# Row fetches by byte offset, sixteen registers a load, three buffers a queue, and more tiles for the SyncE and ScalarE queues

## The chip, the cores and the metric

The kernel runs on one core of one Trainium2 chip. The metric is the device time of one execution in microseconds (us). The engines are PE (TensorE), DVE (VectorE), ACT (ScalarE), POOL (GpSimd) and SP (SyncE); SP only issues DMAs and waits. ACT, SP and POOL each have an instruction queue of their own from which they also issue DMAs.

## What is computed

A graph layer for 12,500 nodes of 256 features and 200,000 edges: a layer norm, then a graph convolution and a linear attention, which are both added to x, then a second layer norm and a mixture of eight experts (two for a token).

```python
xn = layernorm(x)
HW = xn @ W
AHW = segment_sum(edge_weight[:, None] * HW[dst], src, num_segments=12500)
q, k = elu(q) + 1, elu(k) + 1                      # linear attention, 8 heads
out = (q @ (k^T v)) / max(q . sum(k), 1e-6) @ Wproj + bproj
x = x + (AHW + b) + out
x = x + moe(layernorm(x))                          # 8 experts, top 2
```

The change touches the segment sum (called the aggregation below): for every edge a row of HW is read and added, weighted, to the row of its node.

## The kernel before

The edges are first sorted into blocks of 128 nodes and laid out in 1660 tiles of 128 edges; four tiles are a set, so there are 415 sets (TSETS). The rows of HW lie in DRAM as h_table, 12,544 rows of 256 floats, 1024 bytes each. For each tile the 128 rows that its edges name have to come into SBUF, one on each partition. Then PE multiplies a selection matrix, made by DVE from the records of the tile, with these rows (function aggregate, L1266), and DVE adds the result to the block in acc (set_turn, add_tile, L1831).

The rows of most tiles are brought by POOL with one indirect DMA a tile, a gather, into message, which holds four sets (gather_set, L758). POOL may begin set k when PE has done set k - 4. Some tiles, always the last of a set, are brought in another way: SP and ACT each fetch such a tile with 128 single DMAs, one a row, into fetched (fetch_rows, L455). Set SP_SET + 16 i has a tile of SP, 25 in all, and set ACT_SET + 20 i has one of ACT, 19 in all; POOL makes three gathers in these sets and four in the others, 1616 in all. The numbers of the rows lie as integers in fetch_row, one partition for each fetched tile; a queue loads eight of them into registers with one instruction (load_offsets, L47), bounds them (L48), and issues eight DMAs whose source is given by a register.

A tile is fetched in portions. SP's tile i is spread over the 16 sets from 8 + 16 i (fetch_span), 8 rows a set; ACT's over 20 sets, 6.4 rows a set, cut to whole rows. Each portion is issued in loads of eight and a rest. Two buffers a queue are used in turn; the queue waits until PE has used the tile two before.

The fetches are written by hand into the order of work of two long loops, 49 units each. In the K/V part a unit is three sets: PE projects K and V of a pair of blocks between them (project_kv, L1307), ACT takes the exponential and the RELU of K (split_k, L1005 and L1006) and copies V (L1015), DVE joins them (activate, L1954), and PE sums k^T v (context, L1321). Between the sets' work ACT issues the portion of its tile for three sets, after its copy of V. SP waits until V of the last unit but one is made, issues the DMA of xt for a unit (bring_xt, L566), and then its portion for three sets. In the mix part a unit is five sets: PE projects Q (L1377), ACT takes exponential and RELU of Q (split_q, L1034 and L1035), DVE divides (L1998 to L2002), PE multiplies and adds x (L1397 and L1399), and SP brings xt and x (L566, bring_x, L578) and then its portion for five sets. Four sets between the two parts (WEIGHT_FIRST) fold the weights; the last eleven follow the mix part. Later stages, the gate and the experts, aren't touched.

Of the kernel before, what the change touches and what calls it, by code (L numbers as in the profile page):

```python
# [43 lines left out]
def load_offsets(eng, name, row, first, count, top):  # L44

    registers = name if isinstance(name, list) else [eng.alloc_register(f"{name}{i}") for i in range(count)]
    eng.load(registers, row[0:1, first:first + count] if isinstance(first, int) else row[0:1, DynSlice(first, count)])  # L47
    return [eng.snap(r, min_val=0, max_val=top) for r in registers]  # L48


def gps_layer(nc, x, src, dst, edge_weight, gnn_W, gnn_b, mix_Wq, mix_Wkv, mix_Wproj, mix_bproj,
# [1 line left out]
    import concourse.bass as bass  # L53
    from concourse import mybir

    F32, BF16, I32 = mybir.dt.float32, mybir.dt.bfloat16, mybir.dt.int32
    ALU, ACT, AX = mybir.AluOpType, mybir.ActivationFunctionType, mybir.AxisListType.X
    ds = bass.ds
    Offset = bass.IndirectOffsetOnAxis

    P = 128
    N, C = x.shape
    E = src.shape[0]
    KC = C // P
    NB = -(-N // P)
# [3 lines left out]
    EXPERTS, _, HID = ffn_W1.shape  # L69
# [23 lines left out]
    SET, SETS, RING = 4, 4, 8  # L93
# [6 lines left out]
    CONTEXT_SETS, MIX_SETS = 3, 5  # L100
    CONTEXT_FIRST = RING
# [6 lines left out]
    XGROUPS = -(-NB // XG)  # L108
    assert MIX_END < TSETS and TSETS * SET <= TC and 2 * PAIRS == NB and PAIRS % 2 and RING == 2 * SETS

    SP_SPAN, SP_SET = 16, 27
    ACT_SPAN, ACT_SET = 20, 37
    SP_FETCHED = (TSETS - 1 - SP_SET) // SP_SPAN + 1
    ACT_FETCHED = (TSETS - 1 - ACT_SET) // ACT_SPAN + 1
    SP_TILE, ACT_TILE = SP_SET * SET + SET - 1, ACT_SET * SET + SET - 1
    fetched_of = {SP_SET + i * SP_SPAN: (0, i) for i in range(SP_FETCHED)}
    fetched_of.update({ACT_SET + i * ACT_SPAN: (1, i) for i in range(ACT_FETCHED)})
    assert len(fetched_of) == SP_FETCHED + ACT_FETCHED and max(fetched_of) < TSETS
    FETCHED = SP_FETCHED + ACT_FETCHED

    TURN = 7
    TB = 2 * TURN
# [18 lines left out]
    h_table = nc.dram_tensor("h_table", (NB * P, C), F32, kind="Internal").ap()  # L141
# [6 lines left out]
    with ExitStack() as whole:  # L148
        def sem(name):
            return whole.enter_context(nc.semaphore(name))  # L150

        def sb(name, shape, dtype, scope=whole):
            return scope.enter_context(nc.sbuf_tensor(name, shape, dtype))
# [84 lines left out]
        early = ExitStack()  # L238
# [9 lines left out]
        message = sb("message", [P, SETS, SET, C], F32, early)  # L248
        lane = sb("lane", [P, 1], F32, early)
        select = sb("select", [P, 2, SET, P], F32, early)  # L250
        fetched = sb("fetched", [P, 2, 2, C], F32, early)
        fetch_f = sb("fetch_f", [P, FETCHED], F32, early)
        fetch_row = sb("fetch_row", [FETCHED, P], I32, early)
        inputs = ExitStack()
# [3 lines left out]
        found_a = sb("found_a", [P, PART_MAX * P], I32, inputs)  # L258
        found_b = sb("found_b", [P, PART_MAX * P], I32, inputs)
        inputs.close()  # L260
        mix_w = sb("mix_w", [P, KC, C], F32, early)
        ksum = sb("ksum", [P, KC, P], F32, early)
        ctx_t = sb("ctx_t", [P, KC, P], F32, early)
# [45 lines left out]
        bank = [whole.enter_context(nc.psum_tensor(f"bank{i}", [P, 512], F32)) for i in range(8)]  # L309
# [81 lines left out]
        s_fetch_f = sem("s_fetch_f")  # L391
        s_fetch_psum = sem("s_fetch_psum")
        s_fetch_row = sem("s_fetch_row")
        s_fetched = [[sem(f"s_fetched{q}_{i}") for i in range(2)] for q in range(2)]
        s_acc_made = sem("s_acc_made")
        s_select = sem("s_select")
        s_agg = sem("s_agg")
# [41 lines left out]
        LISTED = [64 * len(range(i, K, 4)) for i in range(4)]  # L439
        PARTS = [(0, 1), (1, 5), (5, 9), (9, RSEG)]  # L440

        def gathered_of(k):

            return sum(SET - (n in fetched_of) for n in range(k % SETS, k + 1, SETS))

        def fetch_rows(eng, registers, queue, i, first, end):

            if i >= 2 and first == 0:
                eng.wait_ge(s_agg, {place: k for k, place in fetched_of.items()}[queue, i - 2] + 1)
            at = i + SP_FETCHED * queue  # L450
            for a in range(first, end, 8):
                n = min(8, end - a)
                rows_at = load_offsets(eng, registers[0:n], fetch_row[at:at + 1, :], a, n, NB * P - 1)
                for j in range(n):
                    eng.dma_start(fetched[a + j:a + j + 1, queue, i % 2, :], h_table[ds(rows_at[j], 1), :]).then_inc(s_fetched[queue][i % 2], 16)  # L455

        def fetch_span(eng, registers, queue, span, first_set, end_set):

            for i in range([SP_FETCHED, ACT_FETCHED][queue]):
                begins = CONTEXT_FIRST + i * span  # L460
                first, end = max(first_set, begins), min(end_set, begins + span)
                if first < end:
                    fetch_rows(eng, registers, queue, i, P * (first - begins) // span, P * (end - begins) // span)
# [29 lines left out]
        def _(sp):  # L493
# [83 lines left out]
                else:  # L577
                    sp.dma_start(x_in[:, pair % 2, :, :], x_pairs[pair:pair + 1, :, :, :].rearrange("a p u c -> p (a u) c")).then_inc(s_x_in[pair % 2], 16)  # L578

            row_registers = [sp.alloc_register(f"row_{i}") for i in range(8)]  # L580

            def fetch_ahead(first, end):
                fetch_span(sp, row_registers, 0, SP_SPAN, first, end)
# [252 lines left out]
        def _(act):  # L836
            steps = Steps(act, s_act)
            for r in range(-(-SEG // 4)):
                n = min(4, SEG - 4 * r) * P
# [48 lines left out]
            for k in range(-(-M // BANK_BATCHES)):  # L888
                first, last = k * BANK_BATCHES, min((k + 1) * BANK_BATCHES, M)
# [4 lines left out]
            for i in range(TURNED):  # L894
# [5 lines left out]
                else:  # L900
                    a = (i - SEG) * 4 * P
                    n = min(4 * P, NCOL - a)
# [95 lines left out]
            copy_weights()  # L998


            def split_k(unit, first=False):
                act.wait_ge(s_k_psum, unit + 1)
                if not first:
                    act.wait_ge(s_k, unit)
                act.activation(exp_kq[:, :], bank[4][:, :], ACT.Exp)  # L1005
                act.activation(relu_kq[:, :], bank[4][:, :], ACT.Relu).then_inc(s_k_split, 1)  # L1006
                act.wait_ge(s_v_psum, unit + 1)
                if not first:
                    act.wait_ge(s_ctx, unit)
                made = bank[5][:, :].rearrange("p (u h c) -> p u h c", u=2, h=KC)  # L1010
                if first:
                    act.activation(v_sb[:, 0, :, 0:P], made[:, 0, :, :], ACT.Copy)
                    act.activation(v_sb[:, 1, :, 0:P], made[:, 1, :, :], ACT.Identity, scale=row_ok[:, 1, 0:1]).then_inc(s_v, 1)
                else:
                    act.activation(v_sb[:, :, :, 0:P], made, ACT.Copy).then_inc(s_v, 1)  # L1015
            act.wait_ge(s_late, 2)
            row_registers = [act.alloc_register(f"row_{i}") for i in range(8)]

            def fetch_ahead(first, end):
                fetch_span(act, row_registers, 1, ACT_SPAN, first, end)  # L1020
            for unit in range(PAIRS):
                split_k(unit, first=unit == 0)
                if unit == 0:
                    act.wait_ge(s_fetch_row, 1)
                fetch_ahead(CONTEXT_FIRST + unit * CONTEXT_SETS, CONTEXT_FIRST + (unit + 1) * CONTEXT_SETS)
            fetch_ahead(WEIGHT_FIRST, MIX_FIRST)

            def split_q(g, first=False):
# [83 lines left out]
        def _(pe):  # L1112
# [12 lines left out]
            for b in range(M):  # L1125
# [3 lines left out]
                for g in range(GS):  # L1129
                    at = 2 * (b % BANK_BATCHES * GS + g)  # L1130
# [119 lines left out]
            for i in range(-(-TC // 512)):  # L1250
                n = min(512, TC - 512 * i)
# [3 lines left out]
            def aggregate(k, slot, first=False):  # L1255
                pe.wait_ge(s_select, k + 1)
                pe.wait_ge(s_message[slot % SETS], 16 * gathered_of(k))
                if k in fetched_of:
                    queue, nth = fetched_of[k]
                    pe.wait_ge(s_fetched[queue][nth % 2], 16 * P * (nth // 2 + 1))  # L1260
                if not (first and slot < 2):
                    pe.wait_ge(s_added, k - 1)
                for j in range(SET):
                    ps = bank[(slot % 2) * 2 + j // 2][:, (j % 2) * C:(j % 2 + 1) * C]
                    rows_of = fetched[:, queue, nth % 2, :] if k in fetched_of and j == SET - 1 else message[:, slot % SETS, j, :]
                    last = nc.tensor.matmul(ps, select[:, slot % 2, j, :], rows_of, start=True, stop=True)  # L1266
                last.then_inc(s_agg, 1)

# [26 lines left out]
            pe.wait_ge(s_fetch_f, 1)  # L1295
            nc.tensor.transpose(bank[6][0:FETCHED, 0:P], fetch_f[:, :], ident[:, :]).then_inc(s_fetch_psum, 1)
            pe.wait_ge(s_joined, RSEG)
# [247 lines left out]
        def _(dve):  # L1545
            steps = Steps(dve, s_dve)
            V = nc.vector
# [255 lines left out]
            for m in range(M):  # L1803
# [8 lines left out]
                def between(i):  # L1812
                    if m + 1 < M:
                        find_third(m * STEP + STEP + 1 + i // 3, i % 3)
# [48 lines left out]
            for nth, (a, b) in enumerate(PARTS):  # L1863
# [23 lines left out]
                if nth == 0:  # L1887
                    for i in range(-(-TC // 512)):
                        n = min(512, TC - 512 * i)
# [11 lines left out]
            steps.done(V.tensor_copy(fetch_f[:, 0:SP_FETCHED], records[:, SP_TILE:SP_TILE + (SP_FETCHED - 1) * SP_SPAN * SET + 1:SP_SPAN * SET, 0]))  # L1901
            steps.done(V.tensor_copy(fetch_f[:, SP_FETCHED:FETCHED], records[:, ACT_TILE:ACT_TILE + (ACT_FETCHED - 1) * ACT_SPAN * SET + 1:ACT_SPAN * SET, 0]))
            steps.settle()
# [1 line left out]
            for k in range(RING - 1, RING):  # L1905
                set_turn(k)
            dve.wait_ge(s_fetch_psum, 1)
            V.tensor_copy(fetch_row[:, :], bank[6][0:FETCHED, 0:P]).then_inc(s_fetch_row, 1)

            def block_stats(first_block, j):  # L1910
                steps.done(V.bn_stats(stats[:, j, :], acc[:, first_block + j, 0:C]))
# [53 lines left out]
            for slot in plain_sets(WEIGHT_FIRST, SETS):  # L1965
                if slot == 0:
                    dve.wait_ge(s_ctx, PAIRS)
                    for h in range(KC):
                        at = h * (P + 1)
# [324 lines left out]
```

## Time and profile before

| | us |
|---|---|
| median of three runs | 3787.94 |
| lowest and highest of them | 3780.83, 3790.05 |
| the profiled execution | 3789.91 |
| its span, first to last instruction | 3788.2 |
| mean granted TensorE clock (of 1) | 0.905 |

The profile is of one execution. Times in it count from the start of the span. An engine is busy while an instruction of it computes; instructions that issue DMAs, load registers or wait aren't counted as busy, but the views by line list them, under SPq and ACTq, with their own durations. Idle time is put down to what ended it; "issue" there is a wait for nothing that the profile shows.

### The profile page before, as it was taken

The numbers are of one execution on the slowest core, as the hardware profiler recorded it, in microseconds if no ns is written. First come the engines' busy times: TensorE is split into PE (matmuls) and PEld (weight loads), VectorE is DVE, ScalarE is ACT, GpSimd is POOL, SyncE is SP. The second block draws the span as 40 slices with busy tenths as digits, with TensorE's granted clock in tenths as the row PEclk, the third lists the DMA queues.
The fourth block names the chain that finished last, engine by engine and source line by source line (L and its number), as shares of the span: only waits on it lengthen the run. The fifth ranks groups of instructions, "written<-read, shape, count | busy, mean of one in ns | idle before, by whom it ended". The sixth has DMA issues, their size and how long they took to land. (4 is left out here: it accounts for less than half of the span.)

```text
span 3788.2 us, 70898 instructions
## 1 busy us (share of the span) xinstructions
PE 2773.6 (73%) x16403; PEld 2280.8 (60%) x16408; DVE 2523.3 (67%) x6338; ACT 637.1 (17%) x1335; POOL 2557.6 (68%) x2387
## 2 busy tenths in 40 slices
PE   1457667587777776777777676676663999999998
PEld 1346666366556665555555555555431888888887
DVE  8999999465555555777777777777683544454444
ACT  8312223311111110000000000000032222122221
POOL 7347777677777777777777777777717478744444
PEclk9987878899999999888888889988876999999999
DMA  5957775744444444444444444444383455544443
GB/s 175 303 165 229 232 222 163 228 117 128 127 128 125 127 125 125 130 130 130 130 130 127 127 131 130 130 130 127 107 254 107 74 121 122 111 79 71 71 73 56
DMA packets 357535, 522.47 MB, mean 138 GB/s; under 512 B 59192, under 2 KB 278332, under 8 KB 357180
## 3 DMA queue, kind: packets, MB, share of 16 engines
q0 software_dynamic: 128832, 269.87, 28.0%
q1 hardware_dynamic: 172947, 191.01, 16.6%
q10 hardware_dynamic: 55401, 57.82, 4.9%
q8 instruction: 105, 1.72, 0.2%
q14 instruction: 250, 2.05, 0.2%
HBM read 378.21 MB, written 140.28 MB: 137 GB/s over the span
## 5 line engine op out<-in xcount | busy, mean ns | idle before, releaser
L758 POOL DMA_INDIRECT message<-h_table,records x1616 | 1551.4, 960 | 509.6 <-issue 494.3
L1266 PE MATMUL bank<-message,select 128*128 128x256 f32 x3232 | 919.6, 434 | 552.6 <-issue 268.1
L1266 PEld LDWEIGHTS bank<-message,select 128*128 128x128 f32 x3232 | 660.3, 213 | 767.4 <-issue 367.7
L1823 DVE TENSOR_SCALAR select<-iota_n,records 128x128 f32<-128x128 f32 x1660 | 596.9, 360 | 489.0 <-PE bank L1266 472.2
L1831 DVE TENSOR_TENSOR acc<-acc,bank 128x256 f32 x1660 | 682.6, 411 | 10.0 <-PE bank L1266 6.3
L802 POOL DMA_INDIRECT out<-acc,row_of x224 | 352.2, 1572 | 356.7 <-DVE acc L2239 230.9
L723 POOL DMA_INDIRECT lists<-placed,dest_i x300 | 349.1, 1164 | 200.9 <-ACT placed L935 106.0
L1506 PE MATMUL bank<-w,acc 128*128 x1792 | 407.6, 381 | 8.0 <-DVE acc L2223 7.9
L1493 PE MATMUL bank<-fx_t,acc 128*128 128x256 f32 x1792 | 408.0, 381 | 1.6 <-ACT fx_t L1086 1.6
L1493 PEld LDWEIGHTS bank<-fx_t,acc 128*128 128x128 f32 x1792 | 342.3, 191 | 49.1 <-issue 2.1
L1506 PEld LDWEIGHTS bank<-w,acc 128*128 128x128 f32 x1792 | 333.0, 191 | 50.6 <-issue 9.4
L2235 DVE TENSOR_TENSOR acc<-bank,table 128x256 f32<-128x256 f32 x224 | 84.5, 419 | 336.1 <-PE bank L1506 187.7
L791 POOL DMA_INDIRECT x_sorted<-acc,token_pos x196 | 192.1, 980 | 128.9 <-DVE acc L1940 69.5
L1034 ACT ACTIVATE exp_kq<-bank 128x512 f32<-128x512 f32 x49 | 29.3, 597 | 1155.2 <-PE bank L1377 1111.8
L2223 DVE TENSOR_SCALAR acc<-bank,table 128x256 f32<-128x256 f32 x448 | 190.6, 478 | 44.4 <-PE bank L1493 35.3
L1307 PE MATMUL bank<-w_cat,xt_in 128*128 128x256 f32 x784 | 199.3, 400 | 5.1 <-DMA xt_in<-xt_dram 5.1
L1307 PEld LDWEIGHTS bank<-w_cat,xt_in 128*128 128x128 f32 x784 | 161.2, 206 | 32.9 <-DMA xt_in<-xt_dram 6.6
L1954 DVE SCALAR_TENSOR_TENSOR act_kq<-exp_kq,relu_kq 128x512 f32<-128x512 f32 x98 | 68.0, 694 | 169.3 <-ACT relu_kq L1006 167.0
L1086 ACT ACTIVATE fx_t<-bank 128x512 f32<-128x512 f32 x112 | 66.9, 597 | 643.3 <-PE bank L1480 643.3
L2000 DVE RECIPROCAL relu_kq<-exp_kq 128x512 f32<-128x512 f32 x49 | 164.3, 3353 | 1.7
L1175 PE MATMUL bank<-place_bf,hot_t 98*128 98x4 bf16 x1575 | 48.6, 165 | 130.7 <-DVE hot_t L1731 127.7
L1194 PE MATMUL bank<-hot_w,hot_q 128*128 128x128 bf16 x1575 | 140.6, 266 | 0.0
(315 smaller groups left out, 3512.8 us busy)
## 6 DMA issues: line engine op xcount, KB each, us to landing
fetched<-h_table SPq DMA_DIRECT2D x3200, 1.0 KB
fetched<-h_table ACTq DMA_DIRECT2D x2432, 1.0 KB
rows<-block_dram SPq DMA_DIRECT2D x75, 514.5 KB
acc<-x_sorted SPq DMA_DIRECT2D x112, 260.0 KB, 2.8
message<-h_table,records POOLq DMA_INDIRECT x1616
xt_in<-xt_dram SPq DMA_DIRECT2D x98, 256.0 KB
x_sorted<-blank_rows ACTq DMA_DIRECT2D x42, 390.0 KB
lists<-zeros_list SPq DMA_DIRECT2D x8, 1664.0 KB, 15.4
```

What stands on the lines that cost most here:

```text
L723: pool.indirect_dma_start(out=lists, out_offset=Offset(ap=dest_i[:, c, i:i + 1], axis=0), in_=placed[:, c % 4, i * G8 * PIECES:(i + 1) * G ...
L758: pool.indirect_dma_start(out=message[:, k % SETS, j, :], out_offset=None, in_=h_table, in_offset=Offset(ap=records[:, k * SET + j, 0:1], ...
L791: pool.indirect_dma_start(out=x_sorted[half], out_offset=Offset(ap=token_pos[:, b, k:k + 1], axis=0), in_=acc[:, b, :], in_offset=None).th ...
L802: pool.indirect_dma_start(out=out, out_offset=Offset(ap=row_of[:, ring, j:j + 1], axis=0), in_=fy[:, slot, j, :], in_offset=None, compute_ ...
L1266: last = nc.tensor.matmul(ps, select[:, slot % 2, j, :], rows_of, start=True, stop=True)
L1307: last = nc.tensor.matmul(ps[:, u * C:(u + 1) * C], xt_in[:, half, k, u * P:(u + 1) * P], w_cat[:, k, cols:cols + C], start=(k == 0), stop ...
L1493: last = nc.tensor.matmul(bank[2 + 2 * slot + h // 2][:, h % 2 * 2 * P:(h % 2 + 1) * 2 * P], w1_now[:, slot, k * HID + h * P:k * HID + (h ...
L1506: last = nc.tensor.matmul(bank[6 + slot][:, j * C:(j + 1) * C], hid_t[:, slot, k, j * P:(j + 1) * P], w2_flat[:, ds(expert + k * C, C)], s ...
L1823: return V.tensor_scalar(select[:, k % 2, j, :], iota_n[:, :], records[:, k * SET + j, 1:2].bitcast(F32), records[:, k * SET + j, 2:3].bit ...
L1831: return V.tensor_tensor(to, to, ps, ALU.add)
L2000: steps.done(V.reciprocal(relu_kq[:, :], exp_kq[:, :]))
L2223: last = V.tensor_scalar(hid_t[:, slot, h, :], bank[2 + 2 * slot + h // 2][:, h % 2 * 2 * P:(h % 2 + 1) * 2 * P], table_flat[:, ds(expert ...
```

## The change

The numbers of the rows are multiplied by 1024 when DVE writes fetch_row, so that fetch_row holds byte offsets. The row DMAs read 1024 bytes of a flat byte view of h_table at such an offset, and write a byte view of fetched. One load brings up to sixteen registers. There are three buffers a queue, and the wait is for the tile three before. SP's tiles are spread over 12 sets, every twelfth set having one (33 tiles), ACT's over 14 (28 tiles, the first in set 36); POOL makes 1599 gathers. In the K/V part ACT issues the portion of a unit's first set between the RELU of K and the copy of V, and that of the other two behind the copy.

```diff
-    SP_SPAN, SP_SET = 16, 27
-    ACT_SPAN, ACT_SET = 20, 37
+    SP_SPAN, SP_SET = 12, 27
+    ACT_SPAN, ACT_SET = 14, 36
...
+    FETCHED, FETCH_RING = SP_FETCHED + ACT_FETCHED, 3
...
+        fetched = sb("fetched", [P, 2, FETCH_RING, C], F32, early)
...
+        ROW_BYTES = 4 * C
+        h_bytes = h_table.rearrange("n c -> (n c)").bitcast(U8)
...
-            if i >= 2 and first == 0:
-                eng.wait_ge(s_agg, {place: k for k, place in fetched_of.items()}[queue, i - 2] + 1)
+            if i >= FETCH_RING and first == 0:
+                eng.wait_ge(s_agg, {place: k for k, place in fetched_of.items()}[queue, i - FETCH_RING] + 1)
...
-            for a in range(first, end, 8):
-                n = min(8, end - a)
-                rows_at = load_offsets(eng, registers[0:n], fetch_row[at:at + 1, :], a, n, NB * P - 1)
+            for a in range(first, end, 16):
+                n = min(16, end - a)
+                byte_at = load_offsets(eng, registers[0:n], fetch_row[at:at + 1, :], a, n, (NB * P - 1) * ROW_BYTES)
                 for j in range(n):
-                    eng.dma_start(fetched[a + j:a + j + 1, queue, i % 2, :], h_table[ds(rows_at[j], 1), :]).then_inc(s_fetched[queue][i % 2], 16)
+                    eng.dma_start(fetched[a + j:a + j + 1, queue, i % FETCH_RING, :].bitcast(U8),
+                                  h_bytes[ds(byte_at[j], ROW_BYTES)].unsqueeze(0)).then_inc(s_fetched[queue][i % FETCH_RING], 16)
...
-            def split_k(unit, first=False):
+            def split_k(unit, between, first=False):
...
                 act.activation(relu_kq[:, :], bank[4][:, :], ACT.Relu).then_inc(s_k_split, 1)
+                between()
                 act.wait_ge(s_v_psum, unit + 1)
...
-            row_registers = [act.alloc_register(f"row_{i}") for i in range(8)]
+            row_registers = [act.alloc_register(f"row_{i}") for i in range(16)]
...
-                fetch_ahead(CONTEXT_FIRST + unit * CONTEXT_SETS, CONTEXT_FIRST + (unit + 1) * CONTEXT_SETS)
+                first_set = CONTEXT_FIRST + unit * CONTEXT_SETS
+
+                def first_rows():
+                    if unit == 0:
+                        act.wait_ge(s_fetch_row, 1)
+                    fetch_ahead(first_set, first_set + 1)
+                split_k(unit, first_rows, first=unit == 0)
+                fetch_ahead(first_set + 1, first_set + CONTEXT_SETS)
...
-            V.tensor_copy(fetch_row[:, :], bank[6][0:FETCHED, 0:P]).then_inc(s_fetch_row, 1)
+            V.tensor_scalar(fetch_row[:, :], bank[6][0:FETCHED, 0:P], float(ROW_BYTES), None, ALU.mult).then_inc(s_fetch_row, 1)
```

## Rows read from the trace of the kernel before

**Rows 1.** Head of the page: the span and its instructions.
```profile
span 3788.2 us, 70898 instructions
```

**Rows 2.** Table by stage: busy us (instructions) of each engine, clock, DMA share.
```profile
760.00:1492.00 732.00, 543.39 (x2389) 445.52 (x2388) 402.63 (x1265) 81.78 (x149) 554.81 (x578) 0.94 0.43 125
1520.00:2700.00 1180.00, 832.83 (x3073) 648.27 (x3071) 871.97 (x2160) 53.38 (x97) 894.96 (x935) 0.88 0.43 129
```

**Rows 3.** Page, costliest groups: busy us, mean ns, idle us before, releaser.
```profile
L758 POOL DMA_INDIRECT message<-h_table,records x1616 | 1551.4, 960 | 509.6 <-issue 494.3
```

**Rows 4.** Timeline of POOL, mix part: start us, duration us [idle before].
```profile
1999.14 0.95 POOL L758 DMA_INDIRECT message<-h_table,records  x1 [0.30 <-issue]
...
2027.98 0.95 POOL L758 DMA_INDIRECT message<-h_table,records  x1 [0.30 <-issue]
```

**Rows 5.** Lines L1005 and L1034: duration ns min/median/max, first and last start.
```profile
L1005 ACT ACTIVATE exp_kq<-bank x49: 597/597/599, 763.4 to 1466.9; 128x512 f32<-128x512 f32 x49
...
L1034 ACT ACTIVATE exp_kq<-bank x49: 597/597/598, 1497.4 to 2675.8; 128x512 f32<-128x512 f32 x49
```

**Rows 6.** Waits, 780 to 1490 us: us in total, times, longest.
```profile
ACT exp_kq L1005 <- issue: 471.2, 38, 13.8
```

**Rows 7.** Waits of SP's queue, 780 to 2700 us.
```profile
SPq L578 <- PE bank L1399: 70.5, 36, 4.1
SPq L566 <- PE bank L1307: 25.5, 21, 2.4
SPq L47 <- PE bank L1266: 5.1, 8, 0.8
SPq L472 <- PE bank L1399: 3.2, 1, 3.2
```

**Rows 8.** Timeline of SP's queue in three short windows of the mix part.
```profile
2012.41 0.23 SPq L455 DMA_DIRECT2D fetched<-h_table  x1
...
2012.41 0.64 SPq L455 DMA_DIRECT2D fetched<-h_table  x2
...
2015.49 4.64 SPq L455 DMA_DIRECT2D fetched<-h_table  x9
```

**Rows 9.** Line L455, all row fetches: duration ns, first and last start.
```profile
L455 SPq MOVE fetched<-h_table x3200: 29/29/38, 758.1 to 2691.4; - x189
L455 SPq DMA_DIRECT2D fetched<-h_table x3200: 224/228/332, 758.1 to 2691.5; - x189
L455 SPq FUSED_REGOPS  x2800: 37/37/48, 758.5 to 2691.3; - x187
...
L455 ACTq DMA_DIRECT2D fetched<-h_table x2432: 234/235/552, 766.6 to 2620.5; - x188
```

**Rows 10.** Line L47, SP's loads of eight registers: duration ns.
```profile
L47 SPq TENSOR_LOAD <-fetch_row x400: 692/788/1037, 757.0 to 2687.4; - x134
```

**Rows 11.** Timeline of ACT's queue in two short windows of the mix part.
```profile
2015.29 3.20 ACTq L455 DMA_DIRECT2D fetched<-h_table  x8
...
2015.29 6.11 ACTq L455 DMA_DIRECT2D fetched<-h_table  x9
```

**Rows 12.** Line L47, single loads of ACT: rows 76, 19, 92, 16, 123.
```profile
L47 ACTq TENSOR_LOAD <-fetch_row x1: 750/750/750, 821.0 to 821.0; - x1
...
L47 ACTq TENSOR_LOAD <-fetch_row x1: 2003/2003/2003, 777.6 to 777.6; - x1
...
L47 ACTq TENSOR_LOAD <-fetch_row x1: 598/598/598, 830.1 to 830.1; - x1
...
L47 ACTq TENSOR_LOAD <-fetch_row x1: 1012/1012/1012, 774.8 to 774.8; - x1
...
L47 ACTq TENSOR_LOAD <-fetch_row x1: 1481/1481/1481, 854.1 to 854.1; - x1
```

**Rows 13.** Line L47, ACT's loads from 1520 to 2700 us.
```profile
L47 ACTq TENSOR_LOAD <-fetch_row x191: 762/2046/2222, 1521.8 to 2618.9; - x191
```

More of the change, by code:

```diff
@@ L54, in gps_layer @@
     from concourse import mybir
-    F32, BF16, I32 = mybir.dt.float32, mybir.dt.bfloat16, mybir.dt.int32
+    F32, BF16, I32, U8 = mybir.dt.float32, mybir.dt.bfloat16, mybir.dt.int32, mybir.dt.uint8
     ALU, ACT, AX = mybir.AluOpType, mybir.ActivationFunctionType, mybir.AxisListType.X
@@ L118, in gps_layer @@
     assert len(fetched_of) == SP_FETCHED + ACT_FETCHED and max(fetched_of) < TSETS
-    FETCHED = SP_FETCHED + ACT_FETCHED
+    FETCHED, FETCH_RING = SP_FETCHED + ACT_FETCHED, 3
     TURN = 7
@@ L250, in gps_layer @@
         select = sb("select", [P, 2, SET, P], F32, early)
-        fetched = sb("fetched", [P, 2, 2, C], F32, early)
         fetch_f = sb("fetch_f", [P, FETCHED], F32, early)
@@ L393, in gps_layer @@
         s_fetch_row = sem("s_fetch_row")
-        s_fetched = [[sem(f"s_fetched{q}_{i}") for i in range(2)] for q in range(2)]
+        s_fetched = [[sem(f"s_fetched{q}_{i}") for i in range(FETCH_RING)] for q in range(2)]
         s_acc_made = sem("s_acc_made")
@@ L578, in bring_x @@
                     sp.dma_start(x_in[:, pair % 2, :, :], x_pairs[pair:pair + 1, :, :, :].rearrange("a p u c -> p (a u) c")).then_inc(s_x_in[pair % 2], 16)
-            row_registers = [sp.alloc_register(f"row_{i}") for i in range(8)]
+            row_registers = [sp.alloc_register(f"row_{i}") for i in range(16)]
             def fetch_ahead(first, end):
@@ L1021, in _ @@
             for unit in range(PAIRS):
-                split_k(unit, first=unit == 0)
-                if unit == 0:
-                    act.wait_ge(s_fetch_row, 1)
-                fetch_ahead(CONTEXT_FIRST + unit * CONTEXT_SETS, CONTEXT_FIRST + (unit + 1) * CONTEXT_SETS)
+                first_set = CONTEXT_FIRST + unit * CONTEXT_SETS
[5 more added lines that the diff above has]
+                fetch_ahead(first_set + 1, first_set + CONTEXT_SETS)
             fetch_ahead(WEIGHT_FIRST, MIX_FIRST)
@@ L1259, in aggregate @@
                     queue, nth = fetched_of[k]
-                    pe.wait_ge(s_fetched[queue][nth % 2], 16 * P * (nth // 2 + 1))
+                    pe.wait_ge(s_fetched[queue][nth % FETCH_RING], 16 * P * (nth // FETCH_RING + 1))
                 if not (first and slot < 2):
@@ L1264, in aggregate @@
                     ps = bank[(slot % 2) * 2 + j // 2][:, (j % 2) * C:(j % 2 + 1) * C]
-                    rows_of = fetched[:, queue, nth % 2, :] if k in fetched_of and j == SET - 1 else message[:, slot % SETS, j, :]
+                    rows_of = fetched[:, queue, nth % FETCH_RING, :] if k in fetched_of and j == SET - 1 else message[:, slot % SETS, j, :]
                     last = nc.tensor.matmul(ps, select[:, slot % 2, j, :], rows_of, start=True, stop=True)
```

## The prediction

> **What bounds the kernel now.** The profiled execution took 3789.9 us, its span is 3788.2 [rows 1], 2 us above the median of the three runs (3780.83 to 3790.05); sums are made against 3789.9, and 0.3%, about 11 us, is what a measurement can tell from no change. No engine is full over the span, so I look at the stage that the change touches. The table by stage [rows 2] shows two parts: 760 to 1492 us, where the K/V pass runs beside the aggregation, three sets a unit, and 1520 to 2700 us, where the mix pass does, five sets a unit. POOL is counted busy 76% in both. But before 1606 of 1616 gathers POOL waited for nothing that the profile shows, in all 494.3 us [rows 3]: 0.95 us of gather and 0.30 us to the next; the 24 from 1999.14 to 2027.98 us follow each other in 28.84 / 23 = 1.254 us [rows 4]. POOL is therefore the bound: a set of four gathers is 5.0 us. The first exponentials of the units confirm the pace: 48 steps in 763.4 to 1466.9 us, 14.66 us a unit, and 48 in 1497.4 to 2675.8, 24.55 us [rows 5]. By gathers alone it would be (12 - 0.34) x 1.254 = 14.6 and (20 - 0.56) x 1.254 = 24.4.
>
> What stands close behind POOL decides this change. SP and ACT each issue one DMA a row for the tiles that POOL leaves to them, and the same two queues also bring x and run the activations that the units wait for. ACT's exponential came late from its own queue in 38 of the K/V units [rows 6]: PE had long made K. SP waited for others only 70.5 + 25.5 + 5.1 + 3.2 = 104 us of the 1912 us in both parts [rows 7]. Both queues are some 95% full already, and the change gives them 33 and 28 tiles in place of 25 and 19.
>
> **What it takes from POOL.** 61 tiles in place of 44: 17 gathers fewer, 17 x 1.254 = 21.3 us [rows 4]. If POOL stays the bound that is the whole gain: 3789.9 - 21.3 = 3769. Its pace would be (12 - 3/12 - 3/14) x 1.254 = 14.47 us a K/V unit and (20 - 5/12 - 5/14) x 1.254 = 24.11 us a mix unit. SP's and ACT's work in a unit must fit into these.
>
> **What a row costs SP and ACT now.** On SP, two row DMAs in a run end 0.64 us after the first begins, one takes 0.23 [rows 8]: a row each 0.41 us, 0.228 of it the DMA, the rest two register instructions (37 and 29 ns) and the gaps around them [rows 9]. Nine rows take 4.64 us, the ninth being the first of the next load [rows 8], so a load of eight with its rows takes 4.64 - 0.26 = 4.38 us: 8 x 0.41 = 3.28, 0.79 for the load [rows 10], and 0.31 for the instruction that checks the values and the gaps. On ACT a row step is 0.39 us, and eight with their load take 6.11 - 0.47 = 5.64 [rows 11]: 3.12, 2.05 for the load, 0.47 for the rest (its first DMA after a load is longer).
>
> Why does the same load take 0.79 us on SP and 2.05 on ACT? Because of where it starts. With 16 sets a tile SP starts always at a multiple of 8 rows. With 20 sets ACT's third set boundary is row 19. Its load of eight from row 76 takes 0.75 us, from row 19 2.00; four from row 92 0.60, three from row 16 1.01, five from row 123 1.48 [rows 12]. I read it as 0.4 us a load and 0.2 us for each step, where a step brings four registers if the start and what is left are multiples of four, and else one: 0.4 + 2 x 0.2 = 0.8; 0.4 + 8 x 0.2 = 2.0; 0.6; 1.0; 1.4. It fits all five, and the median of 2.046 over ACT's loads of the mix part [rows 13], most of which start at such rows.
>
> **The change, part by part.**
>
> Byte offsets: the row number no longer has to be multiplied for each DMA. Bounds: nothing goes (0.41 and 0.39 us stay), or both register instructions go (the DMA with one gap, 0.228 + 0.045 = 0.27, and 0.265). I take the middle, the 37 ns instruction and its gap gone: 0.33 on SP, 0.325 on ACT, since the 29 ns MOVE stands before every row DMA and no row of the trace says that it serves the multiplication. The DMA itself keeps its 0.228 us: it moves the same 1024 bytes.
>
> Sixteen registers a load: the 0.4 us falls on 16 rows, not 8, but the steps stay. A load from a good row costs 0.4 + 4 x 0.2 = 1.2 us, from another 0.4 + 16 x 0.2 = 3.6. For the check of sixteen values I add 0.1 us: 0.41 on SP, 0.57 on ACT beside the load.
>
> Twelve and fourteen sets: three sets of twelve are 32 rows, so in the K/V part SP starts at good rows. Five sets are 53.3 rows: mix units start at rows 53, 106, 32, 85, 10 and so on. Counted from the code, 88 of SP's 196 loads there start at a multiple of four, and 2614 rows need 1750 steps (before: 1960 rows, 490 steps). On ACT one set is 9.14 rows; in the K/V part, 1344 rows, 147 loads (the split into one and two sets keeps it at three a unit), 1068 steps.
>
> Third buffer: the wait is then for a set 17 before the first fetched one, and was 13 before. It spares waits of bursts, not work. The multiplication moves into an instruction of DVE that ran once anyway; nothing.
>
> ACT's split: one set's rows stand between the RELU and the copy of V. This takes no time off the queue; what is queued behind them is the copy, and PE waits for it in the unit's third set.
>
> **The sums.** Checked on the old kernel: SP in the mix part 1960 x 0.41 + 245 x (0.4 + 0.31) + 490 x 0.2 + 49 x 0.9 (xt and x) = 1120 us; 49 x 24.55 less SP's waits of some 100 is 1103. It fits.
>
> New, SP in the mix part: 2614 x 0.33 = 863, 196 x (0.4 + 0.41) = 159, 1750 x 0.2 = 350, 49 x 0.9 = 44: 1416 us, 28.9 a unit, where 24.55 went before: 49 x 4.35 = 213 us more. ACT there: 2204 rows, 159 loads, 1571 steps, 49 x 1.2 of activations: 716 + 154 + 314 + 59 = 1243, 25.4 a unit, hidden behind SP. New, ACT in the K/V part: 437 + 147 x 0.97 = 143 + 214 + 59 = 853, 17.4 a unit against 14.66: 134 us more. SP there: 1568 x 0.33 + 98 x 0.81 + 392 x 0.2 + 25 = 699, 14.3 a unit, hidden. The queues don't make it up later: xt of the next unit stands behind the rows on SP, the exponential behind them on ACT, and PE, DVE and at last POOL, which needs the messages' buffers back, wait for those. 3789.9 + 213 + 134 = **4137 us**.
>
> **Rivals.**
>
> *No register instruction goes.* SP mix 1072 + 553 = 1625, 33.2 a unit, +422; ACT K/V 524 + 416 = 940, 19.2, +222: 4434 us. For it: the trace shows no row DMA at a register without both.
>
> *Both go.* SP mix 706 + 553 = 1259, 25.7, +56; ACT K/V 356 + 416 = 772, 15.75, +54: 3900 us. Against it: the MOVE.
>
> *Loads cost the same however many registers and wherever they start* (the other side). With 0.8 us a load, as SP's now, SP mix is 863 + 196 x 1.21 + 44 = 1144, 23.3 a unit, under 24.11; ACT K/V 437 + 147 x 1.37 + 59 = 697, 14.2, under 14.47. POOL stays the bound: 3769. It decides from about 0.9 us a load. Against it stand the loads of 0.6 to 2.0 us [rows 12]; for it, that no load of sixteen is in the trace. The Trainium skill, "DMA: Bandwidth & Descriptors", section "Latency and other measured facts", gives tensor_load a floor of about 600 ns and unrolls four times to share it; by a floor alone, longer loads are the right cure and the time is this rival's 3769. The trace bears out the 0.6 us for four registers, but not that it is all.
>
> *The register row is no longer well placed.* fetch_f, four bytes a fetched tile, grows from 44 x 4 = 176 to 61 x 4 = 244 bytes a partition, and fetch_row lies behind it. Were tiles packed without rounding, SP's K/V loads would go singly too (+217, mix +386): about 4390. Against it: tiles of 4 bytes stand ahead of it now, and loads at multiples of four are quick.
>
> **How the numbers follow.** Forecast 0.50 (its own range 4060 to 4220: 0.02 us on a row is 50 us); no instruction gone 0.18; both 0.10; misplaced row 0.02; POOL stays the bound 0.16; a balance within 11 us 0.04. Slower 0.80, same 0.04, faster 0.16. The range leaves out the faster case: 3785 to 4450.
>
> **What would show it.** In the profile after: POOL's gathers no longer each 1.254 us but in groups with idle time that PE ended; the mix unit 28.9 us and the K/V unit 17.4; SP's row step 0.33 us; SP's loads of sixteen at 1.2 us in the K/V part, and many near 3.6 in the mix part. Wrong if the loads of sixteen stay near 1 us everywhere, or the row step falls under 0.27.

## The result: 4046 us, and the profile after

The changed kernel takes 4046.15 us (median of four runs, 4042.91 to 4046.38), the kernel before 3788.51 (four runs, 3780.83 to 3790.05): ratio 1.0682, 95% interval 1.0664 to 1.0701. It is slower, as forecast, by 258 us where 347 were forecast. The time lies in the stated range, and 14 us below the range of the case that was forecast (4060 to 4220). The mean granted TensorE clock was 0.864 and had been 0.905; the two queues below set the pace with hardly a wait, so it is not PE's speed that was lost.

In the page of the changed kernel, first its head, then two of the costliest groups (busy us, mean ns of one, idle us before, releaser). They answer to [rows 1, 3].

```profile
span 4044.7 us, 69846 instructions
...
L762 POOL DMA_INDIRECT message<-h_table,records x1599 | 1534.3, 960 | 786.6 <-issue 758.3
...
L1386 PE MATMUL bank<-xt_in,w_cat 128*128 128x256 f32 x392 | 145.6, 536 | 280.5 <-DMA xt_in<-xt_dram 280.5
```

POOL has 17 gathers fewer and 17 us less to do, but stands idle 277 us longer. The profile puts that down to "issue". By the start times in the trace, 71 gathers begin more than 2 us after the one before (one did in the kernel before), 280 us over the pace of 1.254 in all, and 68 of them begin 0.8 us after the end of the last matmul of a set: POOL waited for PE to free its buffers. PE waits 280.5 us for xt in the mix part: those are the DMAs that SP issues between its rows.

The first exponential of each unit, L1009 in the K/V part and L1043 in the mix part, by the view of a line (first and last start at the end). They answer to [rows 5].

```profile
L1009 ACT ACTIVATE exp_kq<-bank x49: 597/597/599, 766.0 to 1550.5; 128x512 f32<-128x512 f32 x49
...
L1043 ACT ACTIVATE exp_kq<-bank x49: 597/597/599, 1583.9 to 2947.1; 128x512 f32<-128x512 f32 x49
```

A K/V unit takes (1550.5 - 766.0) / 48 = 16.34 us and was 14.66, a mix unit (2947.1 - 1583.9) / 48 = 28.40 and was 24.55. That is 48 x 1.69 = 81 and 48 x 3.85 = 185 us. The stretch behind the last of these exponentials is 14.8 us shorter (1097.6 for 1112.4), the stretches before and between them 5.5 longer: 81 + 185 - 15 + 5.5 = 256.5, the whole difference of the two spans.

What SP's queue waited for from 1584 to 2947 us, the mix part (us in total, times, longest), answering to [rows 7]:

```profile
SPq L47 <- PE bank L1275: 5.1, 6, 1.3
SPq L582 <- PE bank L1408: 0.2, 1, 0.2
```

5 us in 1363: SP is the bound there. The waits in the K/V part, 780 to 1550 us:

```profile
ACT exp_kq L1009 <- issue: 437.2, 42, 11.8
...
PE bank L1330 <- ACT v_sb L1020: 211.9, 47, 7.3
```

There it is ACT: 42 exponentials came late from its own queue (38 did before [rows 6]), and PE waits in 47 of the units for V, whose copy now stands behind rows. By the start times in the trace, ACT's queue stood 8.8 us in all at its activations in these 770 us, and 80 us in the kernel before (780 to 1466): it is full now, and was some 88% full, not the 95% that the prediction gave both queues.

How the rows are issued, first by line L458 (durations in ns, min/median/max), then by SP's timeline in two windows that begin together (16 DMAs, and 17, the last of the next load). They answer to [rows 8, 9].

```profile
L458 SPq MOVE fetched<-h_table x4224: 29/29/38, 759.0 to 2973.2; - x192
L458 SPq DMA_DIRECT2D fetched<-h_table x4224: 224/228/488, 759.1 to 2973.2; - x192
L458 ACTq MOVE fetched<-h_table x3584: 29/29/35, 766.0 to 2953.0; - x200
L458 ACTq DMA_DIRECT2D fetched<-h_table x3584: 234/235/550, 766.1 to 2953.3; - x200
```

```profile
2016.65 5.13 SPq L458 DMA_DIRECT2D fetched<-h_table  x16
...
2016.65 7.19 SPq L458 DMA_DIRECT2D fetched<-h_table  x17
```

The FUSED_REGOPS of 37 ns is gone, the MOVE and the 228 ns of the DMA stayed. A row costs (5.13 - 0.23) / 15 = 0.327 us in this load, 0.322 in its undisturbed steps, and 0.333 on the mean of SP's mix part, where some steps, mostly those next to a load, are longer.

The loads, line L47, of SP's and ACT's queue from 780 to 1550 us, then of both from 1584 to 2947 us, answering to [rows 10, 13]:

```profile
L47 SPq TENSOR_LOAD <-fetch_row x97: 1149/1227/1451, 785.6 to 1544.7; - x97
...
L47 ACTq TENSOR_LOAD <-fetch_row x141: 765/1264/3844, 781.1 to 1548.7; - x141
...
L47 SPq TENSOR_LOAD <-fetch_row x189: 779/1391/3802, 1584.1 to 2941.8; - x189
...
L47 ACTq TENSOR_LOAD <-fetch_row x158: 597/3212/4003, 1583.9 to 2938.1; - x158
```

In the K/V part all of SP's loads of sixteen start at multiples of four and take 1.2 us; elsewhere loads of sixteen reach 3.6 to 4.0.

### The profile page after: what moved, and what is told of

The parts are those of the page before. It is cut to its first block and busy times, and to the rows that moved or that the text cites. A ratio compares the mean times of both kernels' runs of the same rounds, so it can differ in the third digit from the quotient of the medians.

```text
span 4044.7 us, 69846 instructions
## 1 busy us (share of the span) xinstructions
PE 2831.3 (70%) x16403; PEld 2348.9 (58%) x16408; DVE 2522.6 (62%) x6338; ACT 639.2 (16%) x1335; POOL 2538.8 (63%) x2370
## 5 line engine op out<-in xcount | busy, mean ns | idle before, releaser
L762 POOL DMA_INDIRECT message<-h_table,records x1599 | 1534.3, 960 | 786.6 <-issue 758.3
L1275 PE MATMUL bank<-message,select 128*128 128x256 f32 x3198 | 871.6, 424 | 78.3 <-DVE acc L1840 52.3
L1275 PEld LDWEIGHTS bank<-message,select 128*128 128x128 f32 x3198 | 682.3, 218 | 227.5 <-DVE select L1832 96.0
L1386 PE MATMUL bank<-xt_in,w_cat 128*128 128x256 f32 x392 | 145.6, 536 | 280.5 <-DMA xt_in<-xt_dram 280.5
L1995 DVE TENSOR_TENSOR acc<-acc,bank 128x512 f32<-128x512 f32 x49 | 33.7, 687 | 428.0 <-ACT relu_kq L1044 427.9
L1386 PEld LDWEIGHTS bank<-xt_in,w_cat 128*128 128x128 f32 x392 | 100.6, 268 | 315.9 <-DMA xt_in<-xt_dram 297.4
L1330 PE MATMUL bank<-v_sb,act_kq 128*128 128x129 f32 x388 | 95.1, 422 | 216.0 <-ACT v_sb L1020 215.6
L1043 ACT ACTIVATE exp_kq<-bank 128x512 f32<-128x512 f32 x49 | 29.3, 597 | 1339.4 <-PE bank L1386 893.3
L1330 PEld LDWEIGHTS bank<-v_sb,act_kq 128*128 128x128 f32 x388 | 82.3, 313 | 234.2 <-issue 234.2
L1316 PE MATMUL bank<-w_cat,xt_in 128*128 128x256 f32 x784 | 189.0, 384 | 0.0
```

The source lines that it names most:

```text
L762: pool.indirect_dma_start(out=message[:, k % SETS, j, :], out_offset=None, in_=h_table, in_offset=Offset(ap=records[:, k * SET + j, 0:1], ...
L1316: last = nc.tensor.matmul(ps[:, u * C:(u + 1) * C], xt_in[:, half, k, u * P:(u + 1) * P], w_cat[:, k, cols:cols + C], start=(k == 0), stop ...
L1386: last = nc.tensor.matmul(bank[4][:, o * C:(o + 1) * C], w_cat[:, k, 2 * C + o * P:2 * C + (o + 1) * P], xt_in[:, half, k, :], start=(k == ...
```

## The experiments

Each ran in turns with the kernel before on one chip; the ratio is to that. The units are worked out from the first and last exponential of each run, as above.

| run | us | ratio (95%) | K/V unit | mix unit |
|---|---|---|---|---|
| the change | 4046.2 | 1.0682 (1.0664 to 1.0701) | 16.34 | 28.40 |
| e1 portions at multiples of 4 | 3767.5 | 0.9947 (0.9931 to 0.9964) | 14.42 | 24.35 |
| e2 kernel before, odd starts | 4118.3 | 1.0876 (1.0858 to 1.0895) | 17.07 | 29.02 |
| e3 no split | 4018.0 | 1.0611 (1.0593 to 1.0629) | 15.81 | 28.42 |
| e4 old spans | 3788.3 | 1.0005 (0.9995 to 1.0014) | 14.56 | 24.52 |
| e5 SP 12, ACT 20 sets | 3978.3 | 1.0506 (1.0488 to 1.0523) | 14.49 | 28.79 |
| e6 SP 16, ACT 14 sets | 3904.3 | 1.0310 (1.0293 to 1.0328) | 16.42 | 25.43 |
| e7 multiples of 16, 10 and 12 sets | 4102.4 | 1.0835 (1.0817 to 1.0853) | 17.06 | 28.85 |
| e8 = e1 with two buffers | 3767.4 | 0.9949 (0.9933 to 0.9966) | 14.40 | 24.45 |
| e9 = e1 with loads of eight | 3861.4 | 1.0192 (1.0175 to 1.0209) | 15.13 | 25.74 |
| e10 = e1 with row numbers | 4127.7 | 1.0887 (1.0869 to 1.0906) | 17.13 | 29.18 |

**e1, good starts.** The changed kernel; only the borders of the portions are cut down to multiples of four rows.

```diff
-                    fetch_rows(eng, registers, queue, i, P * (first - begins) // span, P * (end - begins) // span)
+                    fetch_rows(eng, registers, queue, i, P * (first - begins) // span // 4 * 4, P * (end - begins) // span // 4 * 4)
```

> The changed kernel, but each portion begins and ends at a row that is a multiple of four; as many rows and tiles. Theory (the start of a load decides, SP is the bound in the mix part, ACT in the K/V part): SP in the mix part needs 2616 x 0.322 + 196 x 0.81 + 654 steps x 0.2 + 44 = 1176 us, 24.0 us a unit, ACT in the K/V part 12.9, both under POOL's 24.1 and 14.5; so 3765 to 3800 us, SP's long loads at 1.2 us and none at 3.6. Rival (39% more rows are too many for these queues, however they are loaded): 4000 us or more. Rival (the rows between RELU and the copy of V make V late): the K/V unit stays at 16.3, 3850 to 3880 us.

Measured: 3767.5 us, 0.9947 of the kernel before: 0.5% under it, little but clear of the interval, and 279 us under the changed kernel. Its loads by line L47, and then POOL's gathers in its table of groups:

```profile
L47 SPq TENSOR_LOAD <-fetch_row x297: 557/1225/1472, 756.1 to 2676.3; - x149
L47 ACTq TENSOR_LOAD <-fetch_row x284: 583/1202/1477, 761.3 to 2658.2; - x142
```

```profile
L762 POOL DMA_INDIRECT message<-h_table,records x1599 | 1533.3, 959 | 504.7 <-issue 488.9 <-DVE records L1895 12.2 <-PE bank L1275 3.7
```

No load is over 1.48 us, and POOL is idle 504.7 us in place of 786.6. As many rows, tiles and loads on SP (ACT has 284 loads for 309): the 279 us between this kernel and the changed one come from where portions begin and end. The split stays in it, and V no longer comes late.

But SP has no slack left. Its queue's waits from 780 to 2700 us:

```profile
SPq L47 <- PE bank L1275: 9.4, 10, 1.3
SPq L582 <- PE bank L1408: 0.5, 1, 0.5
SPq L570 <- PE bank L1316: 0.2, 1, 0.2
```

That is 10 us in 1920. With 0.333 us a row, not the 0.322 of the expectation, SP needs 24.6 us a mix unit, half a us over POOL's 24.1: here SP and POOL are about level.

**e2, bad starts for the kernel before.** Everything as before the change, but the rows stand one integer further right in fetch_row.

```diff
-        fetch_row = sb("fetch_row", [FETCHED, P], I32, early)
+        fetch_row = sb("fetch_row", [FETCHED, P + 4], I32, early)
...
-                rows_at = load_offsets(eng, registers[0:n], fetch_row[at:at + 1, :], a, n, NB * P - 1)
+                rows_at = load_offsets(eng, registers[0:n], fetch_row[at:at + 1, :], 1 + a, n, NB * P - 1)
...
-            V.tensor_copy(fetch_row[:, :], bank[6][0:FETCHED, 0:P]).then_inc(s_fetch_row, 1)
+            V.tensor_copy(fetch_row[:, 1:P + 1], bank[6][0:FETCHED, 0:P]).then_inc(s_fetch_row, 1)
```

> The kernel before, with its 8 registers a load, row numbers and spans; only the rows stand one integer further to the right in their partitions, so that no load of eight of SP begins at a multiple of four. Theory: SP's loads of eight go from 0.79 to 2.0 us; SP needs 28.9 us a mix unit and 17.3 us a K/V unit, 49 x 4.3 + 49 x 2.6 = 340 us more: 4080 to 4140 us. Rival (the start of a load doesn't matter, ACT's loads are slow because they are ACT's): within 15 us of 3789.

Measured: 4118.3 us. SP's loads of eight, which took 0.79 us [rows 10]:

```profile
L47 SPq TENSOR_LOAD <-fetch_row x400: 1837/1947/2145, 756.1 to 3055.6; - x134
```

Nothing but the position changed, and each of 400 loads takes 1.16 us more, as on ACT: the start of a load decides, not the queue. 400 x 1.16 = 464 us of work on SP became 332 us of time; of the rest, 104 us are SP's waits of before [rows 7], and some 20 the lead of SP that is described below.

**e3, no split.** ACT's portion in one piece again, behind the copy of V.

```diff
                 def first_rows():
                     if unit == 0:
                         act.wait_ge(s_fetch_row, 1)
-                    fetch_ahead(first_set, first_set + 1)
-                split_k(unit, first_rows, first=unit == 0)
-                fetch_ahead(first_set + 1, first_set + CONTEXT_SETS)
+                split_k(unit, lambda: None, first=unit == 0)
+                first_rows()
+                fetch_ahead(first_set, first_set + CONTEXT_SETS)
```

> The changed kernel with ACT's portion of a K/V unit in one piece behind the copy of V, as before the change. Theory (ACT's own work is the bound there): 105 loads in place of 147 and 1011 steps in place of 1068, ACT needs 15.3 us a unit in place of 16.3: 49 us less, 3985 to 4010 us; the mix unit stays at 28.4. Rival (the rows ahead of the copy make PE wait for V): the K/V unit goes back to POOL's 14.5, 3950 to 3965 us. Rival (the split is worth having): 4060 us or more.

Measured: 4018.0 us; the K/V unit 15.81. Most of the part's loss stays without the split, so V's place in the queue is not the cause; the split costs some 28 us here through its extra loads. The unit is 0.5 us above what was expected; that I didn't resolve.

**e4, the old number of tiles.**

```diff
-    SP_SPAN, SP_SET = 12, 27
-    ACT_SPAN, ACT_SET = 14, 36
+    SP_SPAN, SP_SET = 16, 27
+    ACT_SPAN, ACT_SET = 20, 37
```

> The changed kernel with 16 and 20 sets a tile as before: 25 and 19 tiles, 1616 gathers; byte offsets, sixteen registers, three buffers and the split stay. Theory: SP needs 18.2 us a mix unit and 11.1 a K/V unit, ACT 17.8 and 11.2, all far under POOL's 24.4 and 14.6; POOL is the bound as before: 3780 to 3795 us, no gain for the cheaper rows. Rival (one of the other parts slows by itself: the byte view, the split): 3820 us or more.

Measured: 3788.3 us, no change. ACT's loads are still long there (median 3.1 us), but POOL is the bound, and what byte offsets and longer loads save is hidden.

**e5 and e6, one queue at a time.** The same two lines, with 12 and 20 sets (ACT's first in set 36) in e5, 16 and 14 in e6.

> The changed kernel with only SP's tiles at 12 sets, ACT's at 20 as before (33 and 19 tiles, 1608 gathers). Theory: the K/V part is POOL's again at 14.5 us a unit (SP 14.0, ACT 11.2), the mix part stays SP's at 28.4: some 185 us over the kernel before, 3940 to 3980 us. Rival (ACT's rows are what slows both parts): 3780 to 3800 us.

> The changed kernel with only ACT's tiles at 14 sets, SP's at 16 as before (25 and 28 tiles, 1607 gathers). Theory: the K/V part stays ACT's at 16.3 us a unit, some 80 us over the kernel before; in the mix part ACT needs 24.3 us a unit, as much as POOL: 3860 to 3895 us. Rival (SP's rows are what slows both parts): 3770 to 3795 us.

Measured: 3978.3 and 3904.3 us. The exponentials of e5, then of e6:

```profile
L1009 ACT ACTIVATE exp_kq<-bank x49: 597/597/598, 761.5 to 1457.0; 128x512 f32<-128x512 f32 x49
...
L1043 ACT ACTIVATE exp_kq<-bank x49: 597/597/598, 1489.6 to 2871.5; 128x512 f32<-128x512 f32 x49
```

```profile
L1009 ACT ACTIVATE exp_kq<-bank x49: 597/597/597, 766.0 to 1554.2; 128x512 f32<-128x512 f32 x49
...
L1043 ACT ACTIVATE exp_kq<-bank x49: 597/597/598, 1587.3 to 2807.9; 128x512 f32<-128x512 f32 x49
```

SP's tiles slow the mix part alone (28.79 us, K/V 14.49), ACT's the K/V part (16.42), and a little the mix part (25.43). There too the exponentials of e6 come late from ACT's own queue (1590 to 2800 us):

```profile
ACT exp_kq L1043 <- issue: 1060.6, 43, 27.4
```

So ACT's work in a mix unit is 25.4 us and not the 24.3 of the expectation, which had rows and loads cheaper than they are there. That the prediction's sum gives 25.4 too is luck: its 1.2 us of activations, 0.1 in the trace, make up for the same rows and loads. The time is 9 us above the range expected.

**e7, good starts and still more tiles.** Portions at multiples of sixteen, 10 and 12 sets a tile.

```diff
-    SP_SPAN, SP_SET = 12, 27
-    ACT_SPAN, ACT_SET = 14, 36
+    SP_SPAN, SP_SET = 10, 27
+    ACT_SPAN, ACT_SET = 12, 36
...
-                    fetch_rows(eng, registers, queue, i, P * (first - begins) // span, P * (end - begins) // span)
+                    fetch_rows(eng, registers, queue, i, P * (first - begins) // span // 16 * 16, P * (end - begins) // span // 16 * 16)
```

> Portions that begin and end at multiples of sixteen rows, so that every load starts well, but still more tiles: 10 and 12 sets a tile, 39 and 32 tiles, 1589 gathers. Theory (what a queue has to issue in a unit is the sum of its rows, loads and steps): SP needs 16.7 us a K/V unit and 27.4 us a mix unit, above POOL's 14.4 and 23.9; 48 x 2.0 + 48 x 2.85 = 230 us more than before, 3990 to 4030 us. Rival (with good starts the rows are hidden): 27 gathers fewer, 3750 to 3760 us.

Measured: 4102.4 us, above what was expected; the units are 17.06 and 28.85. SP's queue from 780 to 2900 us waited for this:

```profile
SPq L47 <- PE bank L1275: 2.0, 2, 1.1
```

SP was never idle, so the direction holds, and good starts alone are not enough. The units are 2% and 5% above the sums (16.7 and 27.4). The mix sum was added up too low: 64 rows at 0.322, four loads at 0.41 + 1.2 and 0.9 for xt and x are 27.95. The other 0.9 us are the prices: by the start times in the trace a row took 0.33 us there and a load with its check 1.68, 28.8 in all.

**e8, two buffers.** e1 with `FETCH_RING` at 2.

> The kernel of portions at multiples of four (12 and 14 sets a tile) with two buffers a queue in place of three. Theory: the third buffer carries little; a tile's first portion then waits for a set 5 (SP) or 0 (ACT) before its own, so ACT stalls for a set or two in every 14 and has 1.5 us a unit to spare: 3770 to 3830 us. Rival (the buffers decide): 3900 us or more. Rival (they do nothing): 3762 to 3772 us.

Measured: 3767.4 us, as e1. The third buffer does nothing that can be measured; the stalls that I expected for ACT did not come to anything.

**e9 and e10, the two other parts taken back.** e1 with loads of at most eight, and e1 with row numbers.

```diff
-            for a in range(first, end, 16):
-                n = min(16, end - a)
+            for a in range(first, end, 8):
+                n = min(8, end - a)
```

```diff
-                    eng.dma_start(fetched[a + j:a + j + 1, queue, i % FETCH_RING, :].bitcast(U8),
-                                  h_bytes[ds(byte_at[j], ROW_BYTES)].unsqueeze(0)).then_inc(s_fetched[queue][i % FETCH_RING], 16)
+                    eng.dma_start(fetched[a + j:a + j + 1, queue, i % FETCH_RING, :], h_table[ds(byte_at[j], 1), :]).then_inc(s_fetched[queue][i % FETCH_RING], 16)
...
-            V.tensor_scalar(fetch_row[:, :], bank[6][0:FETCHED, 0:P], float(ROW_BYTES), None, ALU.mult).then_inc(s_fetch_row, 1)
+            V.tensor_copy(fetch_row[:, :], bank[6][0:FETCHED, 0:P]).then_inc(s_fetch_row, 1)
```

> The kernel of portions at multiples of four (12 and 14 sets a tile) with loads of at most eight registers. Theory: each load has some 0.7 us beside its steps, so more loads push SP over POOL: 15.2 to 15.6 us a K/V unit, 25.7 to 26.5 a mix unit, 3850 to 3910 us. Rival (with good starts the loads are hidden): 3762 to 3775 us.

> The kernel of portions at multiples of four (12 and 14 sets a tile) with row numbers in place of byte offsets; sixteen registers stay. Theory: the FUSED_REGOPS is back before each row DMA, 0.41 and 0.39 us a row, SP needs 16.8 to 17.2 us a K/V unit and 28.7 to 29.4 a mix unit: 4050 to 4120 us. Rival (the byte offsets save an instruction that was hidden): 3762 to 3800 us.

Measured: 3861.4 and 4127.7 us. In e10, by line L458, the instruction is back, which names what the byte offsets save:

```profile
L458 SPq FUSED_REGOPS  x3927: 37/37/48, 760.7 to 3051.2; - x197
```

Both parts do what they say, 94 and 360 us with SP at its limit, where e1 already has it. In e4 both together were worth nothing.

## Why the prediction was right, and where its sizes were off

The bound: right. POOL gave up its place to SP in the mix part and to ACT in the K/V part, as the waits, e5 and e6 show.

The price of a load: right. 0.4 us and 0.2 us a step, read from five loads of up to eight, held for sixteen registers: 1.2 us from a good row, 3.6 to 3.8 from another. e1 and e2 show it from both sides. One wording is off: nine loads of ten from a multiple of four took 1.26 us on SP (median), two steps of four and two single ones, so the start alone has to be a multiple of four, and not what is left as well; the prediction's counts of 1750 and 1068 steps go by the start. The rival of a fixed price for a load falls: loads go to 4.0 us. The floor of some 600 ns that the Trainium skill gives ("DMA: Bandwidth & Descriptors", section "Latency and other measured facts") is about the price of four well placed registers (0.60 us, and 0.557 the shortest in e1). It is no floor here: DVE's 415 loads of four from another table (tile_row) have a median of 0.342 us in the trace of the changed kernel. For longer loads, too, the measurement decides.

The row step: right, the middle case. One instruction went and the MOVE stayed: 0.333 us a row on SP's mean, where I took 0.33. The time alone could not have told it from the rival in which both go (4046 lies 91 us from 4137 and 146 from 3900); the lines of L458 do. What was held for the other rival, that no row DMA stands without both instructions, was misread: [rows 9] has 2800 FUSED_REGOPS for 3200 row DMAs.

Of the 90 us that the forecast was too high, 53 are the K/V part's, 28 the mix part's, and 9 lie in the stretches around them.

The mix part: SP's price was right, and a term was missing. These are SP's DMAs of xt in the mix part, first before the change, then after it, then in e5:

```profile
L566 SPq DMA_DIRECT2D xt_in<-xt_dram x49: 362/363/363, 1469.0 to 2647.3; - x49
```

```profile
L570 SPq DMA_DIRECT2D xt_in<-xt_dram x49: 359/363/363, 1550.3 to 2940.1; - x49
```

```profile
L570 SPq DMA_DIRECT2D xt_in<-xt_dram x49: 359/363/363, 1475.5 to 2864.4; - x49
```

After the change SP goes round in (2940.1 - 1550.3) / 48 = 28.95 us, and 28.9 was forecast for it. The exponentials follow at 28.40 because SP entered the part with a lead and used it up: the xt of a unit was issued 33.6 us ahead of its exponential in the first unit (1550.3 and 1583.9), 7.0 in the last (2940.1 and 2947.1). These 26.6 us are nearly all of the 28. Before the change the lead was 28 us at both ends. In e5, where ACT doesn't hold up the K/V part, SP goes at the same 28.94 but begins with a lead of 14.1 us, and so its mix unit is the longer one, 28.79. The sum took the pace of the queue for the pace of the part.

The K/V part: the mis-sized term is ACT's 1.2 us of activations a K/V unit, 59 us in the sum: forecast 17.4 us a unit, measured 16.34. The activations hardly hold up the queue. ACT's timeline shows an exponential, and line L47 the load behind it:

```profile
1010.03 0.60 ACT L1009 ACTIVATE exp_kq<-bank 128x512 f32<-128x512 f32 x1 [10.77 <-issue]
1010.52 0.59 ACT L1010 ACTIVATE relu_kq<-bank 128x512 f32<-128x512 f32 x1
```

```profile
L47 ACTq TENSOR_LOAD <-fetch_row x1: 2162/2162/2162, 1010.1 to 1010.1; - x1
```

The load begins at 1010.1, while the exponential runs from 1010.03 to 1010.63 and the RELU has not begun. By the start times in the trace the exponential and the RELU take 0.11 us of the queue, the copy of V 0.08. With 0.19 us in place of 1.2 the same sum gives 437 + 143 + 214 + 9 = 803, 16.4 a unit, and 16.34 was measured.

The end of the sum: I took the loss of both parts and left the rest as it was. The stretch behind the last mix exponential is 15 us shorter in the changed kernel, and between 1095 and 1106 us in e2, e3, e5, e6, e7, e9 and e10, all bound by SP or ACT. 12 of the 15 us lie ahead of POOL's last gather. A likely reason, only argued, is that POOL, waiting with full buffers, has gathers ready when the rows end; but e8, which loses nothing, has 1103 too, so this stays open.

The split costs a little (e3), the third buffer nothing (e8), the place of fetch_row was good: SP's K/V loads were quick.

## What to carry to other kernels

Before a queue is given more work, add up what it issues in one unit of the loop, instruction by instruction, and set it against the engine that bounds the loop now: in the mix part this was decided by 29 us of SP against 24 of POOL, on queues that no busy share counts. A queue that was ahead eats up its lead before its pace becomes the pace of the loop. When such a portion is cut by a ratio, look at where the pieces begin: cutting them to multiples of four made the same change 279 us faster, and a gain of 0.5% out of a loss of 6.8%. A saving off the bound is worth nothing by itself (e4) and much once its queue is the bound (e9, e10).

## What was not expected of the hardware

That a register load costs by where it begins was read from the trace; that the rule holds unchanged for sixteen, and that shifting a table by four bytes costs a whole kernel 8.8% (e2), was not expected to be so exact. And ACT's queue goes on to the next register load within 0.1 us of handing over an activation of 0.6 us.
